# Graph attention in a 512-node model: own edges taken from SBUF, biases as rows of the edge product, its start split in four, owner words loaded between the splits

## The reference, cut to what matters

```
mean_ea = segment_sum(edge_attr, dst) / max(cnt, 1)
ea2 = concatenate([edge_attr, mean_ea])
for k in range(3):
    xl = x @ Wl[k] + bl[k]
    xr = x @ Wr[k] + br[k]
    ef = ea2 @ We[k]
    m = leaky_relu(xl[src2] + xr[dst2] + ef, 0.2)
    logit = m @ att[k]
    alpha = segment_softmax(logit, dst2)
    out = segment_sum(xl[src2] * alpha[:, None], dst2) + b_out[k]
    h = out + x
    x = relu(layernorm(h) * gamma[k] + beta[k])
```

## Time and profile before

| | us |
|---|---|
| median of 3 runs (2296.2 to 2300.84) | 2299.2 |
| the profiled execution | 2290.56 |
| its span, first to last instruction | 2288.8 |
| graph attention, all three layers (about 606 to 1345 us of the span) | 739 |
| of these, the three stretches of `edge_products` and `edge_logits` | 134, 128, 132 |

### The profile page before, as it was taken

How to read it: one execution, slowest core, us unless ns; L and a number is a source line. 1 busy time by engine, 2 the same in 40 slices (tenths; PEclk the granted TensorE clock), 3 DMA queues, 4 the chain that set the end, 5 groups by cost and what they waited for, 6 DMA issues and landing times. The chain is left out here.

```text
span 2288.8 us, 28562 instructions
## 1 busy us (share of the span) xinstructions
PE 1975.8 (86%) x9123; PEld 1031.7 (45%) x9159; DVE 986.7 (43%) x2938; ACT 492.4 (22%) x1238; POOL 346.7 (15%) x363
## 2 busy tenths in 40 slices
PE   8798988999578788978888779869789999979994
PEld 4354557777233233323332233324434444468783
DVE  6454453000367786878677861136421111031111
ACT  0143441111222350125012512127110000010000
POOL 0000001333136302640254000000000000010002
PEclk9899998999789889998999899989999999989997
DMA  0202029984456304540354459954341220079882
GB/s 27 83 1 93 1 93 376 375 326 179 110 172 171 101 1 153 161 129 1 101 147 131 148 182 381 387 200 162 103 168 70 78 78 0 0 270 389 314 310 89
DMA packets 181009, 358.22 MB, mean 157 GB/s; under 512 B 28912, under 2 KB 38400, under 8 KB 180864
## 3 DMA queue, kind: packets, MB, share of 16 engines
q1 hardware_dynamic: 156128, 281.97, 34.6%
q0 software_dynamic: 24736, 74.34, 11.1%
HBM read 334.17 MB, written 22.09 MB: 156 GB/s over the span
## 5 line engine op out<-in xcount | busy, mean ns | idle before, releaser
L1350 POOL DMA_INDIRECT w<-xl_d,src_i x228 | 234.1, 1027 | 404.8 <-DMA xl_d<-XL 261.1
L1005 PEld LDWEIGHTS ps<-tokT,w 128*128 128x128 f32 x2304 | 259.8, 192 | 11.3 <-issue 7.8
L1005 PE MATMUL ps<-tokT,w 128*128 128x128 f32 x2304 | 260.6, 275 | 3.8 <-DVE tokT L1106 2.9
L1463 PE MATMUL ps<-w,oht 128*128 x660 | 195.6, 401 | 46.0 <-issue 37.1
L1554 ACT ACTIVATE w<-ps 128x512 f32<-128x512 f32 x114 | 65.7, 597 | 368.9 <-PE ps L1468 151.2
L1463 PEld LDWEIGHTS ps<-w,oht 128*128 128x128 bf16 x684 | 60.9, 100 | 176.7 <-issue 154.3
L1468 PE MATMUL ps<-w,ident 128*128 128x512 f32 x228 | 126.3, 636 | 4.5 <-issue 4.4
L1159 POOL DMA_INDIRECT spread_d<-N,slot x12 | 11.8, 984 | 726.1 <-DVE slot L1078 723.0
L1019 PE MATMUL ps<-w,O 128*128 128x512 f32 x256 | 111.2, 592 | 0.0
L1691 DVE SCALAR_TENSOR_TENSOR w<-w,att 128x512 f32<-128x512 f32 x114 | 78.2, 686 | 66.1 <-ACT w L1554 46.5
L1714 DVE SCALAR_TENSOR_TENSOR M<-pen,L,M 128x128 bf16 x228 | 79.1, 347 | 31.2 <-issue 26.8
(11 more groups left out here) (465 smaller groups left out, 3107.2 us busy)
## 6 DMA issues: line engine op xcount, KB each, us to landing
w<-L_ffn_W SPq DMA_DIRECT2D x16, 2048.0 KB
w<-L_ffn_W SPq DMA_DIRECT2D x8, 4096.0 KB
w<-fc1T SPq DMA_DIRECT2D x32, 1024.0 KB, 14.3
w<-fc2T SPq DMA_DIRECT2D x32, 1024.0 KB, 14.5
w<-L_ffn_w_gate SPq DMA_DIRECT2D x20, 1024.0 KB
w<-L_ffn_w_up SPq DMA_DIRECT2D x20, 1024.0 KB
w<-L_ffn_w_down SPq DMA_DIRECT2D x10, 2048.0 KB
w<-L_ffn_w SPq DMA_DIRECT2D x8, 2048.0 KB, 12.7
```

What stands on the lines that cost most here:

```text
L1005: m = pe.matmul(k.ps[:, 1 + (q * ins + i) % 4, s * P:(s + 1) * P], self.W1[u][i][:, f, (q * T + s) * P:(q * T + s + 1) * P], self.tokT[:, ...
L1350: gp.indirect_dma_start(self.G[:, i % FAR_AHEAD, :], None, k.xl_d, bass.IndirectOffsetOnAxis(ap=k.src_i[:, i:i + 1].bitcast(U32), axis=0)) ...
L1463: m = pe.matmul(bank, self.oht[:, i * P:(i + 1) * P], self.XP[:, q].rearrange("p t n -> p (t n)")[:, bass.ds(at, D)], start=False, stop=(q ...
```

## The change

- The 4 tiles of own edges come first. Their source rows are the rows of XL in SBUF, so they are not gathered: 72 indirect DMAs a layer in place of 76, and the first of them is tile 4 (`source`, `landed`, `linear`). Their owner is known when the program is written, so `at` needs no register for them.
- The sum bl + br enters the edge product as three more rows (15 in place of 12, with ones in the turned attributes). XL and xr carry no bias any more; `b_out` gets `bl` added once. One broadcast load a layer (`br`) goes; the small table of rows takes 28 DMAs at the start in place of 24, and three loads feed it in place of one.
- PE finishes xl bank by bank (t outermost), ACT copies each bank to XL as it comes, and DVE does the residual rows in three steps between the dot products (`base`). `split3` on xr starts from PSUM and has four instructions in place of six with the bias.
- DVE loads its 10 owner words in pieces: 3 before the last dot product, 2 after it, then 2, 2 and 1 between the splits of xr.
- In the graph convolution PE loads its words (10) at the start of its block, ahead of the turning.

```diff
+    GROUPS = (0, 6, 12, 17, JOBS)
...
+        if i < T:
+            return width * i
...
-        for dst, m in ((self.bl[:], k.i["L1_gnn_bl"][l]), (self.br[:], k.i["L1_gnn_br"][l]),
+        for dst, m in ((self.bl[:], k.i["L1_gnn_bl"][l]),
...
-                             k.we_d[q].rearrange("(l c n) -> c l n", l=3, c=2)).then_inc(self.we_loaded.sem, 16)
+                             k.we_d[q, 3 * D:9 * D].rearrange("(l c n) -> c l n", l=3, c=2)
+                             ).then_inc(self.we_loaded.sem, 16)
+            sp.dma_start(self.we[32 * g + 12:32 * g + 15, :, :], k.we_d[:, 0:3 * D].rearrange("q (l n) -> q l n", l=3)
+                         ).then_inc(self.we_loaded.sem, 16)
...
-            for i in range(EA):
-                if i >= FAR_AHEAD:
+            for i in range(T, EA):
+                u = (i - T) % FAR_AHEAD
+                if i >= T + FAR_AHEAD:
                     gp.wait_ge(self.product.sem, self.product.at(EA * l + i - FAR_AHEAD + 1))
                     gp.wait_ge(self.linear.sem, self.linear.at(self.QUADS * l + (i - FAR_AHEAD) // QUAD + 1))
-                gp.indirect_dma_start(self.G[:, i % FAR_AHEAD, :], None, k.xl_d,
+                gp.indirect_dma_start(self.G[:, u, :], None, k.xl_d,
                                       bass.IndirectOffsetOnAxis(ap=k.src_i[:, i:i + 1].bitcast(U32), axis=0)
-                                      ).then_inc(k.pool_slot[i % FAR_AHEAD].sem, 16)
+                                      ).then_inc(k.pool_slot[u].sem, 16)
...
+        if i >= T:
+            u, n = (i - T) % FAR_AHEAD, (i - T) // FAR_AHEAD + 1
+            slot = self.k.pool_slot[u]
+            eng.wait_ge(slot.sem, slot.at(16 * (l * ((EB - u + FAR_AHEAD - 1) // FAR_AHEAD) + n)))
+
+    def source(self, i):
+
+        return self.XL[:, i, 0:D] if i < T else self.G[:, (i - T) % FAR_AHEAD, 0:D]
...
-        for f in range(T):
-            if f == 0:
-                pe.wait_ge(self.matrix[0].sem, self.matrix[0].at(16 * (l + 1)))
-            pe.wait_ge(self.cols.sem, self.cols.at(T * l + f + 1))
-            for t in range(T):
+        pe.wait_ge(self.matrix[0].sem, self.matrix[0].at(16 * (l + 1)))
+        for t in range(T):
+            for f in range(T):
+                if t == 0:
+                    pe.wait_ge(self.cols.sem, self.cols.at(T * l + f + 1))
                 m = pe.matmul(k.ps[:, T + t, :], k.NT[:, f, t * P:(t + 1) * P], self.W[0][:, f, :],
                               start=(f == 0), stop=(f == T - 1))
-                if f == T - 1:
-                    m.then_inc(self.xl_done.sem, 1)
+            m.then_inc(self.xl_done.sem, 1)
             if l == 0:
-                if f == 0:
-                    pe.wait_ge(self.cols.sem, self.cols.at(T))
+                if t == 0:
                     pe.wait_ge(self.dst_rows.sem, self.dst_rows.at(1))
-                at = [0, 6, 12, 17, self.JOBS]
-                self.jobs(pe, at[f], at[f + 1])
+                self.jobs(pe, self.GROUPS[t], self.GROUPS[t + 1])
...
-                pe.matmul(k.ps[:, (i + T) % DEEP, :], self.eaT[32 * g:32 * g + 12, q * P:(q + 1) * P],
-                          self.we[32 * g:32 * g + 12, l, :], start=True, stop=False)
+                pe.matmul(k.ps[:, (i + T) % DEEP, :], self.eaT[32 * g:32 * g + 15, q * P:(q + 1) * P],
+                          self.we[32 * g:32 * g + 15, l, :], start=True, stop=False)
...
-                    m = pe.matmul(bank, k.ident[:], self.G[:, i % FAR_AHEAD, 0:D], start=False, stop=True)
+                    m = pe.matmul(bank, k.ident[:], self.source(i), start=False, stop=True)
...
-            if l == 0:
-                self.empty_jobs(a)
+            for t in range(T):
+                a.wait_ge(self.xl_done.sem, self.xl_done.at(T * l + t + 1))
+                a.activation(self.XL[:, t, 0:D], k.ps[:, T + t, :], ACT.Copy).then_inc(self.rows_copied.sem, 1)
+                if l == 0:
+                    self.empty_jobs(a, self.GROUPS[t], self.GROUPS[t + 1])
...
     def biases(self, v, l):
 
         k, ch = self.k, self.ch
-        v.wait_ge(self.vectors.sem, self.vectors.at(96 * (l + 1)))
+        v.wait_ge(self.vectors.sem, self.vectors.at(80 * (l + 1)))
         for q in range(2):
             last = v.scalar_tensor_tensor(self.xr[:, q, :], self.web[:, q, :], 0.2, self.att[:], ALU.mult, ALU.mult,
                                           accum_out=self.wc[:, q:q + 1])
         ch.link(last)
         v.tensor_scalar(self.att8[:], self.att[:], 0.8, None, ALU.mult)
+        v.tensor_tensor(self.b_out[:], self.b_out[:], self.bl[:], ALU.add)
         ch.link(v.tensor_scalar(self.eac[:], k.ea[:, :, 0], self.wc[:, 0:1], None, ALU.mult))
         ch.link(v.memset(self.M[:], -NEG))
         ch.link(v.scalar_tensor_tensor(self.eac[:], k.ea[:, :, 1], self.wc[:, 1:2], self.eac[:], ALU.mult, ALU.add))
-        v.wait_ge(self.turned.sem, self.turned.at(T * (l + 1)))
-        if l:
-            v.wait_ge(self.gain_rows.sem, self.gain_rows.at(32 * l))
-            for j, op in ((0, ALU.mult), (1, ALU.add)):
-                for t in range(T):
-                    last = v.tensor_tensor(k.N[:, t, :], k.N[:, t, :], self.gain[:, j, :], op)
-                ch.link(last)
+
+    def base(self, v, l, step):
+
+
+        k, ch = self.k, self.ch
+        if step == 0:
+            v.wait_ge(self.turned.sem, self.turned.at(T * (l + 1)))
+            if l:
+                v.wait_ge(self.gain_rows.sem, self.gain_rows.at(32 * l))
         for t in range(T):
-            if l:
-                last = v.scalar_tensor_tensor(k.N[:, t, :], k.N[:, t, :], 0.0, self.b_out[:], ALU.max, ALU.add)
+            rows = k.N[:, t, :]
+            if step < 2:
+                if l:
+                    last = v.tensor_tensor(rows, rows, self.gain[:, step, :], (ALU.mult, ALU.add)[step])
+            elif l:
+                last = v.scalar_tensor_tensor(rows, rows, 0.0, self.b_out[:], ALU.max, ALU.add)
             else:
-                last = v.tensor_tensor(k.N[:, t, :], k.N[:, t, :], self.b_out[:], ALU.add)
-        ch.link(last)
+                last = v.tensor_tensor(rows, rows, self.b_out[:], ALU.add)
+        if l or step == 2:
+            ch.link(last)
 
     def source_rows(self, v, l):
         k, ch = self.k, self.ch
         for t in range(T):
-            v.wait_ge(self.xl_done.sem, self.xl_done.at(T * l + t + 1))
-            ch.link(v.tensor_tensor(self.XL[:, t, 0:D], k.ps[:, T + t, :], self.bl[:], ALU.add))
+            if t < 3:
+                self.base(v, l, t)
+            else:
+                words = self.words(v, 0, 3)
+            v.wait_ge(self.rows_copied.sem, self.rows_copied.at(T * l + t + 1))
             v.scalar_tensor_tensor(self.xr[:, t % 2, :], self.XL[:, t, 0:D], 0.2, self.att[:], ALU.mult, ALU.mult,
                                    accum_out=self.XL[:, t, D:D + 1]).then_inc(self.rows_ready.sem, 1)
+        words += self.words(v, 3, 5)
         for t in range(T):
-            xr = self.xr[:, t % 2, :]
+            rest, bank, parts = self.xr[:, t % 2, :], k.ps[:, t, :], [self.XP[:, q, t, :] for q in range(3)]
             v.wait_ge(self.xr_done.sem, self.xr_done.at(T * l + t + 1))
-            ch.link(v.tensor_tensor(xr, k.ps[:, t, :], self.br[:], ALU.add))
-            split3(v, ch, [self.XP[:, q, t, :] for q in range(3)], xr, xr).then_inc(self.xr_parts.sem, 1)
-
-    def edge_logits(self, v, l):
+            ch.link(v.tensor_copy(parts[0], bank))
+            ch.link(v.tensor_tensor(rest, bank, parts[0], ALU.subtract))
+            ch.link(v.tensor_copy(parts[1], rest))
+            v.tensor_tensor(parts[2], rest, parts[1], ALU.subtract).then_inc(self.xr_parts.sem, 1)
+            if t < T - 1:
+                words += self.words(v, len(words), min(EW, len(words) + 2))
+        return words
+
+    def edge_logits(self, v, l, words):
         k, H = self.k, EA // 2
-        words = self.words(v)
...
-            s = (i - QUAD) % FAR_AHEAD
-            v.tensor_tensor(self.part[:], self.G[:, s:s + QUAD, D], self.eac[:, i - QUAD:i], ALU.add
+            s = (i - QUAD - T) % FAR_AHEAD
+            own = self.XL[:, :, D] if i == QUAD else self.G[:, s:s + QUAD, D]
+            v.tensor_tensor(self.part[:], own, self.eac[:, i - QUAD:i], ALU.add
...
             @block.tensor
             def _(pe):
+                words = [pe.value_load(k.words[0:1, w:w + 1], min_val=0, max_val=P * T ** WORD - 1)
+                         for w in range(EW)]
                 for t in range(T):
                     pe.wait_ge(k.conv_normed.sem, k.conv_normed.at(t + 1))
                     for f in range(T):
@@ -2271,13 +2307,11 @@
                 pe.wait_ge(k.loaded.sem, k.loaded.at(32))
                 pe.wait_ge(k.conv_cols_v.sem, k.conv_cols_v.at(2))
                 pe.wait_ge(k.conv_cols_a.sem, k.conv_cols_a.at(2))
-                words = [pe.value_load(k.words[0:1, w:w + 1], min_val=0, max_val=P * T ** WORD - 1)
-                         for w in range(EB // WORD)]
```

79 lines of the change are left out of this document (40 added, 39 removed).

## The result

The changed kernel took 2275.6 us (median of 4 runs, 2269.6 to 2285.7) against 2299.9 us: ratio 0.990, 95 % interval 0.9868 to 0.9932. The forecast was 2285, with the range 2270 to 2297. Its profiled execution took 2275.97 us (span 2274.3), the one of before 2290.56. From the starts and ends of each stage the two traces divide like this.

A forecast was written before the change was run, and what follows sets the result against it. In the edge stage PE was taken to lead in the middle and DVE at the end. Terms -3 - 6 + 0 - 4.7 = -13.7 us took 2299.2 to 2285.5, stated as 2285, range 2270 to 2297.

The forecast's parts named there:

- Part 1: Start of second and third layers: shorter splits with loads between make XP ready earlier, -1.5 us a layer, -3 in two.
- Part 2: End of the edge stage: DVE follows PE from the first tile, some 10 us earlier; 2 us a layer, 6 in all.
- rival (c): Edge stages: DVE's late start is fully on the path; 28.5 us in three layers, -33 with convolution, 2266; chance 0.18.
- Part 3: Start of the first layer: last split -2.7 us, or +2.3 if a stop of 5 us falls there; taken as 0.
- Part 4: Graph convolution: with word loads ahead of the turning, PE clears its banks at 1540.3 instead of 1544.99, -4.7 us.
- Rival (a): Edge stages: stops set their length and only change place; only the convolution's -4.7 us remains, 2294.5; chance 0.16.
- Rival (b): Layer starts: loads between splits stop at 1.84 us each, +4.1 a layer; +7.6 in all, 2306.8, slower; chance 0.06.

The follow-up runs named there:

- group 1: First group of follow-up kernels, on one chip: the changed kernel again, three variants of it, and the kernel before at 2295.9 us.
- ctl_after: Changed kernel run again, nothing edited: 2281.0 us, ratio 0.9913 to the kernel before.
- e4: Changed kernel with xr's split made from an SBUF copy of the bank, five operations in place of four: 2285.4 us, ratio 0.9927 to the kernel before.
- ctl_before: Kernel before run again, nothing edited: 2295.9 us, ratio 0.9989.
- e2: Changed kernel with DVE's ten owner-word loads back in one line behind the last split: 2279.6 us, ratio 0.9927 to the kernel before.
- e9: Changed kernel with PE's adjacency words ahead of the minima wait and DVE's words in one line behind the last split: 2196.3 us, 0.9908 of before.
- b1: Kernel before with one edit, the convolution's owner-word loads at the head of PE's part of the block: 2294.6 us, ratio 0.9983.
- e6: Changed kernel with one gather for every four edge tiles, 18 a layer in place of 72: 2203.9 us, ratio 0.9946 to the kernel before.
- e7: Changed kernel with already-met waits added on PE and DVE, restoring the earlier instruction positions: 2204.7 us, ratio 0.9954 to the kernel before.
- e8: Changed kernel with own edges last again, still read without a gather: 2204.5 us, ratio 0.9946 to the kernel before.
- e1: Changed kernel with the convolution's ten word loads put back behind the turning and copies: 2281.0 us, ratio 0.9924 to the kernel before.

## Why the prediction came out as it did

**The total** was right in size: -13.7 forecast, -24.3 by the medians of the first comparison and -14.9 in group 1. The parts were right less often than the total, and that it fits so well is luck: the edge stages won by a way that no term had, and unchanged code gave back 10 us.

**Part 1** held. XP is ready 2.2 us and 1.9 us earlier in the pair and 1.5 to 2.0 in ctl_after, with -1.5 a layer forecast; the split's 2.60 us, the rate of the loads and DVE waiting for PE are as worked out. Its count of a bank, 3.2 us of work under 3.5 of cover, comes out too: in the first layer, where DVE does not wait, the splits with two loads between them start 3.2 us apart. How much hangs on this thin margin is shown by e4, which adds 0.9 us a bank (3.5 for 2.6) and loses 3.2 to 4.6 us a layer.

**Part 2** is the step that failed: "DVE can now follow PE from the first tile" was to shorten the lag before L1475 by 6 of 28.5 us. The lag was 29.7, 26.3 in ctl_after and 26.7 in ctl_before, and e2 and e9 take the head start away at no cost. The stages did become shorter, by 10 us in the pair and 16 on average, but among the products: 365.2, 371.8 and 382.4 us in the order before and 346.5 to 364.1 in the seven traces of the changed one. PE's stops that count as issue were 38.5 us in each of the two traces of before, 46.3 in b1, and 24.6 to 34.7 in the seven (the wait for XP ahead of a layer's first product is left out; some traces put it down to issue too, and the 28.9, 40.1 and 38.8 us of e6's expectation have it in them). Why they are fewer is open. The change takes 19 register instructions a layer from PE and 11 from DVE inside the stage; e7 and e8 were made to test place and order and met a chip without stops. The forecast's text had said against itself that DVE catches up in the middle (rows 4); that argument was the stronger one, and rival (c) is ruled out by the same measurement.

**Part 3** was taken at 0 and was -3.9 in the pair (-3.6 in ctl_after): a term of the sum that was mis-sized. Its own count of DVE's work was right. It had the last split end 2.7 us earlier and then allowed for a stop of 5 us, which did not come; the four splits with their loads took 664.87 - 653.37 = 11.5 us, as counted. The faster xr product, which no term had, is not the cause, as e1 and ctl_after show. With Parts 1 and 3 the layer starts won 9.4 us for the 3 forecast; 1.4 of these are xl's product of the second layer, which ran at the higher clock in that trace by chance.

**Part 4** was right in its block, -5.6 at the first product for -4.7, with the turning 1.4 us later as worked out, and then incomplete: five of the microseconds are lost behind the block, at a lower clock. No term of the forecast looked at unchanged code.

**Rival (a)**, that the gain ends in the convolution, had a part of the truth, but the other way round: it kept only the convolution's gain, and that is the part that hardly reached the end. Rival (b), the loads between the splits, is real from 3.5 us a bank on, and did not occur.

**The rule weighed.** The Trainium skill (Runtime: NRT & Kernel Launch, Instruction fetch mechanics) has instructions brought in ahead, with the boundaries mostly hidden. On the third chip the trace agrees, with ten loads in 6.1 us (e9) and 1.1 us of stops a layer. On the first chips ten loads took 12.1 us (e2) and PE's stops 25 us and more. Whether that goes against the rule depends on whether these stops are late instructions, and no run here shows it. The profile's two queues of instructions do not tell the chips apart: 88 packets of 1.44 MB with 0.3 % of the DMA time in one, 57 packets with 0.1 % in the other, in before and in e7 alike.

By subtraction, the kernel before needs about 318 us in its edge stages on the third chip: 2214.5, less 1.7 around the span, less 1895 for all else as its traces have it. That is 7 us above e7's, with an error of about 5 (an estimate; no trace of the kernel before was taken there).

## What to carry to other kernels

Before a few microseconds are read from a pair of traces, have a second trace of the same code: here the edge stages moved by 5 to 6 us by themselves, the layer starts by 0.1 and 2.6. And see whether an engine is waited for before its faster product is called a gain. Give a split, a copy or a load that shares a producer's pace its budget per bank, since everything beyond it is multiplied by the banks. And look for small loads on the controlling engine that stand behind a long wait instead of ahead of it; moving TensorE's owner words there was the surest gain of the study, 2 us in each of two layers by moving one line.

## What the runs showed of the hardware that was not expected

- Between the groups the time differed in one stage and hardly elsewhere. Each group had a chip of its own, so the chip and the hour cannot be told apart. The kernel before took 2296 and 2299 us on the chips of the first two groups and 2214.5 on the third's. The changed order's edge stages took 379 to 390 us and 309 to 312, while in the traces of the changed order with the words first the stretches between and behind the blocks agreed within 4 us. On the slower chips PE, DVE and ACT pause together. In the first layer of after ACT starts none of its relus from 695.6 to 705.2 us, though PE makes products in between, DVE idles 5.9 us before 705.9, and from 701.3 PE starts a matmul every 1.1 to 1.4 us, where those of a tile's three parts followed one another every 0.22. ACT has 6 or 7 idle times of over 4 us in each of after's stages behind its first tile, and none in e9's.
- The granted clock of PE depended on the order of work far from the place where it fell: 666.4 to 667.1 us behind the convolution with its word loads late, 670.8 to 674.8 with them early, and for xr's product of the first layer, behind the same pause of 1.9 to 2.0 us, 17.0 us in the three traces of the order before and 13.97 (7 traces) or 15.67 (4) in the changed one.
